# Softmax scaling moved to the heads' output, and the experts' output alternating between two PSUM banks

## The reference

```python
def _L1_attn_ref(x, Wq, Wk, Wv, Wp, bp):         # H, HS = (6, 16)
    q = jnp.einsum('btc,hcd->bhtd', x, Wq)        # k and v alike
    scores = jnp.einsum('bhtd,bhsd->bhts', q, k) * Cx ** (-0.5)
    scores = jnp.where(causal, scores, NEG_INF)
    weights = jax.nn.softmax(scores, axis=-1)
    out = jnp.einsum('bhts,bhsd->bhtd', weights, v)
    catted = out.transpose(0, 2, 1, 3).reshape(Bx, Tx, -1)
    return catted @ Wp + bp
...
t = t + _L1_attn_ref(_ln_t(t), ...)
t = t + _L1_ffn_ref(_ln_t(t), ...)    # 4 experts, top 2, hidden width 384, gelu
```

## Time and profile before

| what | us |
|---|---|
| median of three runs | 464.43 |
| the three runs | 464.39, 464.43, 466.17 |
| the profiled execution | 466.77 |
| its span in the profile | 465.0 |
| PE, PEld busy | 435.8 (94%), 347.0 (75%) |
| DVE, ACT, POOL busy | 269.5 (58%), 263.6 (57%), 145.8 (31%) |
| one block of the loop | 44.20 |

### The profile page before, as it was taken

The page is one execution under the profiler, slowest core; times in us unless marked ns, Lnnn a source line. Parts: engine busy times, 40 slices in busy tenths (PEclk is TensorE's granted clock), DMA queues, the critical chain, the costliest instruction groups (busy, mean ns, idle before and its releaser), DMA issues.

```text
span 465.0 us, 10797 instructions
## 1 busy us (share of the span) xinstructions
PE 435.8 (94%) x3199; PEld 347.0 (75%) x3199; DVE 269.5 (58%) x954; ACT 263.6 (57%) x740; POOL 145.8 (31%) x309
## 2 busy tenths in 40 slices
PE   6999998759899999999999999999999999999897
PEld 6999996436568777877777778678767877787676
DVE  3888888535525852775277437634763585266424
ACT  2544454336477648664865585567657764865370
POOL 5000000425422542362255315531542254235200
PEclk9999999997999999999999999999999999999999
DMA  8600000021021002101210120022002100200000
GB/s 200 134 0 0 0 0 1 25 68 27 1 61 28 19 15 67 39 0 37 52 30 0 45 51 22 0 51 51 17 0 59 42 0 13 68 22 1 15 4 18
DMA packets 14393, 14.95 MB, mean 32 GB/s; under 512 B 5426, under 2 KB 11412, under 8 KB 14372
## 3 DMA queue, kind: packets, MB, share of 16 engines
q1 hardware_dynamic: 14180, 14.30, 12.3%
q0 software_dynamic: 192, 0.39, 0.3%
HBM read 3.86 MB, written 1.57 MB: 12 GB/s over the span
## 4 chain that ended last, share of the span: by engine, by line
PE 74%; DVE 12%; ACT 5%; issue 5%; SPq 2%; DMA 1%; POOL 1%; DVEq 1%; ACTq 0%; POOLq 0%
PE F L1026 19%; PE T L984 9%; PE A L1005 8%; PE F L1042 4%; PE S L968 4%; PE F L1046 4%; PE F L1043 3%; PE S L970 3%; PE F L1022 3%; PE S L973 2%; DVE c L629 2%; DVE ig L627 2%; ACT tc_sb L471 2%; DVE pt_sb L457 1%; PE M L947 1%
## 5 line engine op out<-in xcount | busy, mean ns | idle before, releaser
L406 POOL TENSOR_SCALAR p_sb<-p_sb,rden 128x128 f32<-128x128 f32 (+1 forms) x192 | 79.3, 427 | 133.4 <-DVE rden L710 131.2
L1026 PE MATMUL F<-w_sb,hid 128*128 128x96 f32 x768 | 101.0, 276 | 0.0
L1026 PEld LDWEIGHTS F<-w_sb,hid 128*128 128x128 f32 x768 | 93.4, 192 | 5.9 <-issue 5.9
L518 ACT ACTIVATE p_sb<-S,nmax 128x128 f32<-128x128 f32 (+1 forms) x192 | 78.8, 425 | 17.4 <-DVE nmax L704 17.3
L704 DVE TENSOR_REDUCE nmax<-S 128x2 f32<-128x512 f32 (+1 forms) x80 | 50.7, 634 | 53.1 <-PE S L973 52.8
L457 ACT COPY pt_sb<-T 128x512 f32<-128x512 f32 (+1 forms) x48 | 26.4, 550 | 69.2 <-PE T L984 69.2
L564 ACT ACTIVATE hid<-F,b_sb 128x512 f32<-128x512 f32 x72 | 49.3, 686 | 8.2 <-PE F L1046 7.5
L1005 PE MATMUL A<-pt_sb,v_cur 128*32 128x128 f32 x576 | 44.2, 284 | 8.4 <-ACT pt_sb L457 4.5
L984 PE MATMUL T<-id_sb,p_sb 128*128 128x128 f32 x288 | 49.3, 290 | 1.4 <-POOL p_sb L406 1.4
L968 PE MATMUL S<-k_bd,q_st 96*128 96x384 f32 (+2 forms) x96 | 38.7, 410 | 4.8 <-DMA k_bd<-k_cur 3.8
L984 PEld LDWEIGHTS T<-id_sb,p_sb 128*128 128x128 f32 x288 | 30.9, 143 | 16.2 <-issue 14.1
(11 more groups left out here) (142 smaller groups left out, 793.8 us busy)
## 6 DMA issues: line engine op xcount, KB each, us to landing
k_bd<-k_cur SPq DMA_DIRECT2D x96, 32.0 KB, 2.0
q_st<-q_cur SPq DMA_DIRECT2D x28, 96.0 KB, 2.2
k_bd<-k_cur SPq DMA_DIRECT2D x96, 16.0 KB, 1.8
t_st<-t_cm SPq DMA_DIRECT2D x7, 192.0 KB, 2.4
out_y<-y_sb SPq DMA_DIRECT2D x7, 192.0 KB, 1.9
x_pad<-in_x SPq DMA_DIRECT2D x2, 612.0 KB, 9.0
w_sb<-in_w SPq DMA_DIRECT2D x1, 576.0 KB
hid<-in_w SPq DMA_DIRECT2D x1, 576.0 KB, 7.5
```

Source lines behind the costliest of these rows:

```text
L406: last = nc.gpsimd.tensor_scalar(p, p, rden[:, u % 3, i:i + 1], 1.0, ALU.mult, ALU.mult)
L518: last = nc.scalar.activation(p_sb[:, u % 3, i * nk:(i + 1) * nk], S[u % 2][:, i * nk:(i + 1) * nk], ACT.Exp, bias=nmax[:, u % 3, i:i + 1] ...
L1026: last = mm(dst[:, e * C:(e + 1) * C], hid[:, c, s * TT:(s + 1) * TT], w2_sb[:, c], start=False, stop=(c == NCH - 1), skip_group_check=True)
```

## The change

The multiplication by the inverse row sums no longer acts on the probabilities but on the heads' output, once per tile.

- `scale` is gone from POOL. PE's transposes wait for the exponentials alone.
- `den` and `rden` hold six heads of two tiles. `recip` runs once per tile (four a block, not ten).
- `spread` (POOL) copies a tile's six inverse sums to `rden_c`, each 16 times, 128 by 96.
- `turn_sums` (PE) turns `rden_c` into bank F2 (`R`) by a matmul with the identity, so that rows are head dimensions and columns tokens.
- `take_spread` (ACT) copies R to `rden_t`, where `heads_out` stood.
- `heads_out` moves to DVE and is a multiplication of bank A by `rden_t`.
- The experts' output goes to F0, F1, F0, F1, and tiles 2 and 3 wait for the combination of the tile two before. The hidden chunks go round F2, A, F0, F1.

```diff
-        L1 = [F[0], A, F[1], F[2]]
-        L2 = [F[0], F[2], F[1], F[2]]
+        L1 = [F[2], A, F[0], F[1]]
+        L2 = [F[0], F[1], F[0], F[1]]
+        R = F[2]
...
-            def scale(n, u):
-                wait_alone(pool, rden_done, NU * n + u + 1)
...
-                    last = nc.gpsimd.tensor_scalar(p, p, rden[:, u % 3, i:i + 1], 1.0, ALU.mult, ALU.mult)
-                last.then_inc(scaled, 1)
+            def spread(n, s, first=False):
+                wait_alone(pool, rden_done, 4 * n + s + 1)
+                if s or not first:
+                    wait_alone(pool, spread_ready, 4 * n + s)
+                nc.gpsimd.tensor_copy(rden_c[:], rden[:, s % 2].unsqueeze(2).to_broadcast((128, HEADS, HS))
+                                      ).then_inc(rden_spread, 1)
...
-            def heads_out(n, s, first=False):
-                act.wait_ge(av_ready, NU * n + TILE_END[s])
+            def take_spread(n, s, first=False):
+                act.wait_ge(spread_ready, 4 * n + s + 1)
                 if s or not first:
-                    act.wait_ge(proj_ready, 4 * n + s)
-                nc.scalar.copy(o_t[:], A[0:C, 0:TT]).then_inc(ot_done, 1)
+                    act.wait_ge(ot_done, 4 * n + s)
+                nc.scalar.copy(rden_t[:], R[0:C, 0:TT]).then_inc(spread_done, 1)
...
+            def recip(n, s):
+                dve.wait_ge(exp_done, NU * n + TILE_END[s])
+                V.reciprocal(rden[:, s % 2], den[:, s % 2]).then_inc(rden_done, 1)
+
+            def heads_out(n, s, first=False):
+                dve.wait_ge(av_ready, NU * n + TILE_END[s])
+                if s or not first:
+                    dve.wait_ge(proj_ready, 4 * n + s)
+                dve.wait_ge(spread_done, 4 * n + s + 1)
+                V.tensor_tensor(o_t[:], A[0:C, 0:TT], rden_t[:], ALU.mult).then_inc(ot_done, 1)
...
             def probs_t(n, u, first=False):
-                pe.wait_ge(scaled, NU * n + u + 1)
+                pe.wait_ge(exp_done, NU * n + u + 1)
...
+            def turn_sums(n, s, first=False):
+                pe.wait_ge(rden_spread, 4 * n + s + 1)
+                if s or not first:
+                    pe.wait_ge(spread_done, 4 * n + s)
+                mm(R[0:C, 0:TT], rden_c[:].rearrange("p r d -> p (r d)"), id_sb[:], start=True, stop=True
+                   ).then_inc(spread_ready, 1)
...
-                        if s == 3:
-                            pe.wait_ge(comb, 16 * n + 8)
+                        if s >= 2:
+                            pe.wait_ge(comb, 16 * n + 4 * s - 4)
...
+                        for s in range(SPB - 1):
+                            if j == TILE_END[s]:
+                                turn_sums(n, s, first)
                         values(n, j - 1, first)
...
                     project_q(n + 1)
+                turn_sums(n, SPB - 1, first)
                 values(n, NU - 1, first)
```

More of the change, by code:

```diff
@@ L197, in hybrid_kernel @@
         av_ready = sem("av_ready")
+        spread_ready = sem("spread_ready")
+        spread_done = sem("spread_done")
+        rden_spread = sem("rden_spread")
         proj_ready = sem("proj_ready")
@@ L421, in body @@
             def body(n, first=False, last=False):
-                scale(n, 0)
                 for j in range(NU):
-                    if j + 1 < NU:
-                        scale(n, j + 1)
+                    for s in range(SPB):
+                        if j + 1 == TILE_END[s]:
+                            spread(n, s, first)
                     if j == EARLY_T0 + 1 and not last:
@@ L514, in exps @@
                     act.wait_ge(pt_ready, NU * n + u - 2)
-                _, t, _ = UNITS[u]
+                a, t, h0 = UNITS[u]
+                s = 2 * a + t
+                if h0 == 0 and (s > 1 or not first):
+                    act.wait_ge(rden_done, 4 * n + s - 1)
                 nk = TT * (t + 1)
@@ L538, in body @@
                         if j == TILE_END[s]:
-                            heads_out(n, s, first)
+                            take_spread(n, s, first)
                     if j in PT_ON_ACT:
@@ L547, in body @@
                         take_x1(n + 1)
-                heads_out(n, SPB - 1, first)
+                take_spread(n, SPB - 1, first)
                 if not last:
@@ L792, in body @@
                         row_max(n, j + 2)
-                    if j + 1 < NU:
-                        recip(n, j + 1)
+                    for s in range(SPB):
+                        if j + 2 == TILE_END[s]:
+                            recip(n, s)
+                        if j == TILE_END[s]:
+                            heads_out(n, s, first)
                     if j not in PT_ON_ACT:
@@ L812, in body @@
                             normalize2(n, s)
+                heads_out(n, SPB - 1, first)
                 attn_residual(n, SPB - 1)
@@ L1037, in expert_hidden @@
                         pe.wait_ge(ot_done, 4 * n + 4)
-                    elif not first:
+                    elif c and not first:
                         pe.wait_ge(comb, 16 * n - 16 + 4 * (c + 1))
```

21 lines of the change are left out of this document (8 added, 13 removed).

## The result

The changed kernel took 472.65 us in the median of 4 runs (471.75 to 473.57), beside 464.44 us for the kernel before in 4 runs (464.39 to 466.17). The ratio is 1.0168, 95% interval 1.0135 to 1.0201: slower by about 1.7%. The profiled execution took 471.75 us, its span is 469.9 us, against 466.77 and 465.0 before. The forecast was 470.7 us with a range of 467.8 to 473.8.

A forecast was written before the change was run, and what follows sets the result against it. PE, running nearly without holes, was taken to bound the kernel. Blocks 1 to 7 at 0.86 us (6.0), block 0 (0.1) and the end (0.2) add 6.3 us to 464.4, giving 470.7 us, range 467.8 to 473.8.

The forecast's parts named there:

- What bounds the kernel: Steady block: PE is busy 43.18 of 44.20 us; POOL's scaling holds it up in two places only, 1.4 us.
- The price of a turn: On PE, one turn of the sums costs 0.22 us, between bounds of 0.12 and 0.3 us.
- Tile 3: Turn between queries and unit 9's values: 0.14 us could be hidden, but POOL's late spread makes the values 0.2 us late.
- DVE, ACT and POOL: Steady blocks: multiplications of about 0.29 us on DVE stay covered, ACT trades copies, POOL's relief helps nobody; cost nothing.
- Block 0: First block: the 1.06 us wait for POOL goes, DVE is next late, turns take back; +0.1 us, ends -1.4 and +0.9.
- The end: Last experts' output: its bias matmul waits for the gelu of chunk 10, costing 0.15 us.
- The sum: Whole kernel: 6.0 + 0.1 + 0.2 = 6.3 us, giving 470.7 us, 1.4% slower.
- The rival of the repeated run: Whole kernel: the change also makes the low-clock stretch more frequent or longer; 8 us, ratio 1.0175; no chance given.
- 1 (0.12 us a turn): On PE, a turn costs what the values' passes cost, 0.12 us; 3.7 us in all, 468.1 us; 14%.
- 3 (room on PE): On PE, turns run in room its busy time hides, so not slower; 463.2 us; 8%.
- 2 (DVE late): Late DVE multiplications hold up copies of units 5 and 7, up to 4.8 us; 472 to 475.5 us; 15%.
- 4: Bank alternation cuts PE and DVE conflicts, or DVE copies run faster when POOL leaves SBUF alone; 469 us; 5%.

The follow-up runs named there:

- the one with pieces in the middle: Kernel before with two pieces of the experts' output moved from units 4 and 5 to ahead of unit 7's values; 461.84 us, ratio 0.9932.
- the repeated run: The changed kernel measured once more, unaltered, beside runs of the kernel before; 471.97 us against 465.85, ratio 1.0145.
- the four unused matmuls: Kernel before with the new bank order plus four turn-sized matmuls a block on constant data, scaling still on POOL; 470.59 us, ratio 1.0114.
- the alternation alone: Kernel before with only the change's bank order and its waits, scaling still on POOL; 466.68 us against 466.4, ratio 1.0013.
- the first attempt at the filling: Kernel before with two pieces of the experts' output moved from the block's start to ahead of unit 7's values; 469.42 us, ratio 1.0076.
- the kernel with both holes filled: Kernel before with experts' pieces moved into both PE waits, units 7 and 8, and tile 2's combination ahead of DVE's last residual; 461.74 us, ratio 0.9928.
- the filled kernel before: Kernel before with 32 and 18 matmuls that compute nothing ahead of block 0, in place of 24 and 6; 467.54 us, ratio 1.0035.
- the filled changed one: Changed kernel with 32 and 18 matmuls that compute nothing ahead of block 0, in place of 24 and 6; 471.73 us, ratio 1.0128.

## Why the prediction was right, point by point

**What bounds the kernel: right.** One engine in its own order. Four matmuls that nobody waits for cost what the change cost, 0.84 us a block.

**The price of a turn: right.** 0.22 us was taken from the distance around a project-out and around the skip matmul; at tile 1 it is 0.22, in the mean of four 0.21. The lower bound, 0.12 us from the passes of the values, is what one pass costs (0.11 to 0.12), not two.

**Tile 3: right in size, wrong in its reason.** The step said that 0.14 us of the turn would be hidden and that POOL's spread, behind tile 2's power, would take that back. The spread ended at 303.30 and the turn began at 303.40, as far behind the start of the last query matmul as that stood behind the one before (0.23 us): POOL held up nobody. What failed was the 0.14. I had taken the 0.23 us between two starts of the queries as the time after which the values could start, and the rest of the 0.37 as a wait for ACT's copy. But in the changed kernel the values start 0.31 to 0.34 us behind a turn, with or without a copy to wait for, while the turn starts 0.23 us behind the queries. At tile 1 too the turn starts 0.64 us behind the six pieces, where the values started 0.73 us behind them. By these rows, going over to the values takes about 0.1 us by itself, and of the supposed 0.14 only 0.02 to 0.05 were cover. Two errors of opposite sign gave the right 0.20.

**DVE, ACT and POOL: right.** No new wait came up on DVE in the steady blocks, though at tile 1 the copy of unit 5 now starts right behind the reciprocal, with no idle time. The estimate that it "fits with little to spare" held with nothing to spare. POOL's lower load made nobody's instructions shorter: DVE's copies take 0.56 and 0.69 us, as in the earlier trace rows. The 0.08 us less of waiting at unit 7 were not foreseen.

**Block 0: small, as forecast, but by a sum that did not hold.** The forecast was +0.1 us. Its own terms do not add up to that: 0.2 and 0.3 us gained, three turns of 0.22 and 0.2 for tile 3 make +0.36. The measured value is -0.2 us (37.17 us against 37.38 from unit 2's scores, neither with a slow stretch; -0.13 where both have 3.4 us of it). The timelines of PE show why, first the changed kernel (again), then the one with pieces in the middle, whose block 0 is that of the kernel before:

```profile
103.01 0.39 PE L991 MATMUL S<-k_bd,q_st 96*128 96x256 f32 x1 [0.93 <-ACT p_sb L529]
...
112.87 0.46 PE L1037 MATMUL F<-id_sb,rden_c 128*96 128x128 f32 x2 [0.61 <-POOL rden_c L414]
...
140.18 0.44 PE L1053 MATMUL F<-b2hl,ones 2*128 2x384 f32 x1
```

```profile
102.78 0.39 PE L968 MATMUL S<-k_bd,q_st 96*128 96x256 f32 x1 [0.93 <-ACT p_sb L518]
...
110.51 0.66 PE L984 MATMUL T<-id_sb,p_sb 128*128 128x128 f32 x4 [0.54 <-POOL p_sb L406]
...
113.83 0.55 PE L984 MATMUL T<-id_sb,p_sb 128*128 128x128 f32 x3 [1.05 <-POOL p_sb L406]
...
140.16 0.43 PE L1022 MATMUL F<-b2hl,ones 2*128 2x384 f32 x1
```

The trace that the forecast was read from has PE at half the clock from 102.6 to 109.4 us, which hid two waits for POOL's probabilities. Without it there are four, 0.23, 0.54, 1.05 and 0.30 us, 2.1 in all, and all of them go. In their place come 0.15 us for ACT, 0.33 for DVE and 0.61 for POOL, 1.1 in all. The gain of 1.0 us is a little more than the four turns. I had looked for what is late next on DVE, and the largest of the new waits is for POOL: tile 1's sums are spread behind tile 0's power, which waits for DVE's statistics. The step named that very queue for tile 3 and did not walk it for block 0. So both the gain and the new waits were read too small, and that the result came out small is luck.

**The end: right.** The gelu of chunk 10 costs 0.15 us as worked out. The projection's wait for the multiplication in place of the copy grew from 0.45 to 0.48 us, the 0.03 of the forecast. The last block from its tile 0 to the final experts' output is 42.49 us, 41.39 before, so +1.10, where 0.86 + 0.18 was the sum.

**The sum.** The six blocks from tile 0 to tile 0 grew by 4.9 us together (0.82 each in the mean; forecast 5.2), the last by 1.1 (forecast 1.04), block 0 by -0.2 (forecast 0.1): 5.8 us. The two profiles that both have 3.4 us of the slow stretch at 103 us, the second of before and the first of after, took 466.27 and 471.75 us, 5.5 apart. Forecast was 6.3. The means differ by 6.6 us and the first four runs of each by 8.2; what lies above 5.8 is scatter or a cost that only unprofiled runs have, and no run tells which. The rival of the repeated run, that the change makes slow stretches longer or more costly, is thus not excluded for up to 1 us; its 1.0175 lies just outside the interval of the 1.0145 measured. The price of a steady block was reasoned; that the total fell so near the middle of the range is in part luck.

**Rivals.** 1 (0.12 us a turn) and 3 (room on PE) fell with the four unused matmuls, 2 (DVE late) with the same run and DVE's timeline, though DVE had no idle time left at tile 1. Of 4, the banks fell with the alternation alone, and faster copies with DVE's timeline.

## What to carry to other kernels

Work taken off an engine that nobody waits for is worth the waits it ends less those that come up behind them, here 1.0 us in block 0 and 0.08 in a steady block; work added to the engine that runs without holes costs its full distance between starts, which can be read beforehand at a similar instruction. Such an engine's holes are found as its waits in one steady block, and moving work of its own into them gave more (0.43 and 0.70 us a block) than relieving its neighbours. A wait shorter than the overlap of the modelled ends is in no list of waits: compare the distance between two starts with the same pair in another block or version, which is how the 0.19 us of POOL were found. And when two profiles are compared, look at the granted clock first and count from behind the last DMA wait. Before moving anything, walk every queue past which a step moves, in the first and the last block too: the first attempt at the filling lost 0.86 us at one place because it pushed a reduction on DVE.

## What the hardware showed that I had not expected

- A float32 matmul with the identity costs PE twice what a transpose of the same tile costs, 0.22 against 0.11 to 0.12 us for 96 weight columns and 128 streamed, from 45.04 and 44.58 us a block.
- In 13 of 14 profiles PE has a stretch of 3.4 or 6.8 us at a granted clock of 0.50 (1.2 GHz of 2.4), at about 87, 103 or 430 us, in one kernel here and in the next there; the kernel with both holes filled has two, at 87 and 428. Its length or place differs between two profiles of the same kernel, and the second profile of after has none. In the kernel with both holes filled PE had waited 0.68 and 0.45 us in the three us before it fell; in the version beside it the same two waits measure 0.67 and 0.45, and there it stayed up. What sets its place is open. More filling matmuls took it out of block 0 but did not remove it: in the filled kernel before it came at 434 us, in the filled changed one at 89.
